# A layer of cross-attention and product-key experts on one core: five tiles of choice in the first stage, one-hots of every fourth block from ScalarE, halved units

## The reference

```
x = x + attention(layernorm(x), ctx, ctx)          # 16 heads of 16, biases, softmax
y = layernorm(x)
xn = y * rsqrt(mean(y*y) + eps) * norm_w
q = (xn @ wq) -> 8 heads x 2 parts x 128
sim = q . keys                                     # 2 x 8 x 64 per token
s1, i1 = top_k(sim[0], 16); s2, i2 = top_k(sim[1], 16)
final_scores, pk = top_k(all 256 sums s1 + s2, 16) # per head
expert = i1 * 64 + i2 at pk                        # one of 4096
hidden = gelu(xn . expert_down[expert]) * relu(final_scores)
x = x + sum over the 8 x 16 choices of hidden * expert_up[expert]
```

## Time and profile before

| what | value |
|---|---|
| median of 3 runs | 1239.93 us (1236.59 to 1240.88) |
| the profiled execution, its own time | 1236.87 us |
| its span | 1235.1 us |
| PE, DVE, ACT, POOL busy | 1061.3, 982.2, 392.6, 535.8 us |
| granted clock of PE, mean | 0.925 of 2.4 GHz |

### The profile page before, as it was taken

One profiled execution on the slowest core, in us unless ns is written; L12 is line 12 of the kernel. 1 busy time (PEld: TensorE's weight loads), 2 busy tenths in 40 slices (PEclk: granted clock), 3 DMA queues, 4 the chain that ended last, 5 costly groups with the idle time before them and its releaser, 6 DMA issues.

```text
span 1235.1 us, 28831 instructions
## 1 busy us (share of the span) xinstructions
PE 1061.3 (86%) x10152; PEld 728.0 (59%) x10152; DVE 982.2 (80%) x4900; ACT 392.6 (32%) x717; POOL 535.8 (43%) x708
## 2 busy tenths in 40 slices
PE   4899987878868685148998999999999999999998
PEld 2444442323213223047777777888878888888887
DVE  4757555959999998588999999999989999964321
ACT  2256544424444361013222222222222222222211
POOL 6320410432111222226565676676766675766400
PEclk9799998888888797557999999999999999999999
DMA  5344313211321100360000000000100010000000
GB/s 167 123 140 142 114 46 121 80 54 42 92 86 41 48 11 26 108 237 2 2 29 16 16 25 16 20 27 9 40 12 25 2 34 16 25 16 24 2 18 9
DMA packets 59925, 63.76 MB, mean 52 GB/s; under 512 B 6882, under 2 KB 56164, under 8 KB 59268
## 3 DMA queue, kind: packets, MB, share of 16 engines
q1 hardware_dynamic: 59780, 61.90, 15.5%
HBM read 42.21 MB, written 19.66 MB: 50 GB/s over the span
## 4 chain that ended last, share of the span: by engine, by line
PE 53%; DVE 26%; POOL 8%; issue 7%; DMA 3%; ACT 2%; SPq 1%; POOLq 0%; DVEq 0%; ACTq 0%
PE bank L1256 50%; DVE mem L1175 4%; POOL mem L783 4%; PE bank L1259 3%; DVE mem L1111 2%; DVE mem L1212 2%; DVE mem L1058 1%; DVE mem L1057 1%; SPq L484 1%; DVE mem L1114 1%; DVE mem L1107 1%; DVE mem L1094 1%; DVE mem L1062 1%; DVE mem L1054 1%; DVE mem L979 1%
## 5 line engine op out<-in xcount | busy, mean ns | idle before, releaser
L1256 PE MATMUL bank<-mem 128*128 128x32 bf16 (+5 forms) x9672 | 1012.3, 276 | 104.2 <-DVE mem L1175 35.6
L1256 PEld LDWEIGHTS bank<-mem 128*128 128x128 bf16 (+3 forms) x9672 | 675.7, 123 | 390.0 <-issue 171.8
L783 POOL TENSOR_TENSOR mem<-mem 128x1536 bf16<-128x1536 bf16 x118 | 325.7, 2761 | 236.4 <-DVE mem L1212 202.7
L1175 DVE TENSOR_REDUCE mem<-bank 128x1 f32<-128x512 f32 x256 | 167.9, 682 | 82.1 <-PE bank L1256 81.9
L888 ACT ACTIVATE mem<-bank 128x512 f32<-128x512 f32 x256 | 148.8, 601 | 203.5 <-PE bank L1256 202.6
L924 ACT ACTIVATE bank<-bank 128x512 f32<-128x512 f32 x128 | 74.5, 582 | 332.3 <-PE bank L1256 332.3
L1212 DVE TENSOR_TENSOR mem<-mem,bank 128x2048 bf16<-128x2048 bf16 x128 | 155.4, 1214 | 0.0
L1259 PE MATMUL bank<-mem 128*128 128x128 f32 (+3 forms) x480 | 75.5, 289 | 66.2 <-POOL mem L695 25.0
L1226 DVE TENSOR_TENSOR mem<-bank,mem 128x512 f32<-128x512 f32 x128 | 87.7, 685 | 49.1 <-ACT bank L924 43.8
L1259 PEld LDWEIGHTS bank<-mem 128*128 128x128 f32 (+3 forms) x480 | 54.9, 142 | 113.5 <-issue 70.8
L932 ACT COPY mem<-bank 128x512 f32<-128x512 f32 x128 | 74.9, 585 | 113.3 <-PE bank L1256 113.3
(11 more groups left out here) (101 smaller groups left out, 678.7 us busy)
## 6 DMA issues: line engine op xcount, KB each, us to landing
mem<-parts_d SPq DMA_DIRECT2D x192, 64.0 KB, 2.3
parts_d<-mem SPq DMA_DIRECT2D x16, 384.0 KB, 2.6
mem<-in_L_ffn_expert_down SPq DMA_DIRECT2D x16, 256.0 KB, 2.8
downT_d<-mem SPq DMA_DIRECT2D x16, 256.0 KB, 3.1
mem<-downT_d SPq DMA_DIRECT2D x4, 1024.0 KB, 8.8
mem<-in_L_ffn_expert_up SPq DMA_DIRECT2D x4, 1024.0 KB, 16.0
tok_d<-mem SPq DMA_DIRECT2D x16, 160.0 KB, 1.8
mem<-tok_d SPq DMA_DIRECT2D x16, 160.0 KB, 2.5
```

The lines of the kernel that those rows point to most:

```text
L783: nc.gpsimd.tensor_tensor(ow[q % 2], i0, i1, ALU.mult).then_inc(ow_rdy, 1)
L1175: nc.vector.tensor_reduce(nmx[g % 2][:, i % TB, i // TB:i // TB + 1], psum[n % 3][:, :], AX.X, ALU.max, negate=True).then_inc(s_max, 1)
L1256: return nc.tensor.matmul(o, l, r, start=first, stop=last)
```

## The change

Four things. `NA` is 5: five tiles are chosen in the first stage, and slots -1, 0 and 1 have five tiles instead of four. Each search, choose and extract is cut into its two rounds, a unit each (34 units of a tile, with the decode a unit of its own), and keys and decode are put at the head of a step, ahead of the one-hots. POOL waits for the small one-hot alone (`oj_rdy`). And the large one-hot of the blocks 3, 7, 11 and 15 of each slot is made by ACT: it negates the 16 high numbers of the block, then for each of its tokens writes |column - number| over 128 columns (`Abs` with the bias from memory), then relu(1 - that) over all 2048; seven tokens in step 1, seven in step 2 and two with the relu in step 3 of each four.

```diff
-        NA = 6
-        TASKS = ([("search", h) for h in range(FH)] +  [("choose", s) for s in range(4)] +
-                 [("keys", 0)] + [("extract", s) for s in range(4)])
+        NA = 5
+        TASKS = ([("search", n) for n in range(2 * FH)] + [("choose", n) for n in range(8)] + [("keys", 0)] +
+                 [("extract", n) for n in range(8)] + [("decode", 0)])
+        HEAD = ("keys", "decode")
+
+        def at_heads(tasks, steps):
+
+            out = []
+            for s, t, kind, i in tasks:
+                s = max(s, out[-1][0]) if out else s
+                if kind in HEAD and out and out[-1][0] == s and s + 1 < steps:
+                    s += 1
+                out.append((s, t, kind, i))
+            return out
...
+        def by_act(q):
+
+            return q % 4 == 3
+
+        def high_of(q):
+
+            return oh[(q - q // 4) % 2]
...
-            run(-1, 3, NA, 4, -1)
+            run(-1, 3, NA, 5, -1)
...
-        FEW = 5
+        FEW = 10
...
-                tasks = [(16 * n // FEW if n < FEW else 16 + 32 * (n - FEW) // (len(tasks) - FEW), *tasks[n][1:])
-                         for n in range(len(tasks))]
+                tasks = at_heads([(16 * n // FEW if n < FEW else 16 + 32 * (n - FEW) // (len(tasks) - FEW), *tasks[n][1:])
+                                  for n in range(len(tasks))], 16 * n_slots)
...
             def weigh(c, par, q):
 
-                pool.wait_ge(oh_rdy, c * 2 + 2)
+                pool.wait_ge(oj_rdy, c + 1)
...
+            FAR = ((), range(0, 7), range(7, 14), range(14, TK))
+
+            def far_from(k, par, q):
+
+                own, step = q // 4 * 4 + 3, q % 4
+                c, n = (k + 1) * 16 + own, (k + 1) * 4 + q // 4
+                if step == 1:
+                    r = 2 * (1 - par) + q // BPT
+                    if q % BPT == 1:
+                        act.wait_ge(tokT_ld[r], ((k + 1) * 2 + q // BPT) * 4 + (16 - 4 * r))
+                    at_least(act, c_mm, c - 3)
+                    nc.scalar.activation(minus, tokT[r][:, own % BPT, 0, :], ACT.Copy, scale=-1.0).then_inc(oh_minus, 1)
+                    act.wait_ge(oh_minus, n + 1)
+                for t in FAR[step]:
+                    nc.scalar.activation(far[:, t, :], row, ACT.Abs, bias=minus[:, t:t + 1]).then_inc(oh_far, 1)
+                if step == 3:
+                    act.wait_ge(oh_far, n * TK + TK)
+                    nc.scalar.activation(far, far, ACT.Relu, bias=1.0, scale=-1.0).then_inc(oh_act, 1)
...
                     if on(kk, 0, 7):
                         gelu(k * 16 + q, q)
+                    if on(kk, -1, 6):
+                        far_from(k, par, q)
...
-                nc.vector.tensor_tensor(oh[q % 2], high.to_broadcast([P, TP, P, PAIR]),
-                                        numbers.unsqueeze(1).to_broadcast([P, TP, P, PAIR]),
-                                        ALU.is_equal).then_inc(oh_rdy, 1)
+                if not by_act(q):
+                    nc.vector.tensor_tensor(high_of(q), high.to_broadcast([P, TP, P, PAIR]),
+                                            numbers.unsqueeze(1).to_broadcast([P, TP, P, PAIR]),
+                                            ALU.is_equal).then_inc(oh_rdy, 1)
...
+                    rest = now["tasks"]
+                    if rest and rest[0][1] in HEAD:
+                        choose_experts(*rest[0])
+                        rest = rest[1:]
                     if on(kk, -1, 6):
                         one_hots(k, par, kk, q)
                     if on(kk1, 0, 7):
                         weigh_hidden(k1, p1, q1)
-                    for task in now["tasks"]:
+                    for task in rest:
                         choose_experts(*task)
...
-                pe.wait_ge(oh_rdy, c * 2 + 2)
+                if by_act(q):
+                    pe.wait_ge(oh_act, (k + 1) * 4 + (q // 4 + 1))
+                else:
+                    pe.wait_ge(oh_rdy, (k + 1) * 12 + (q - q // 4 + 1))
```

More of the change, by code:

```diff
@@ L793, in run @@
                     for tile, kind, i in now["tasks"]:
-                        if (kind, i) == ("extract", 3):
+                        if kind == "decode":
                             weight_parts(tile)
@@ L1100, in make_keys, with extract @@
                 steps.count(nc.vector.tensor_tensor(ik, ik, bits(taken), ALU.bitwise_or))
-            def extract(s):
-                if s == 0:
-                    steps.all()
+            def extract(s, second):
                 both = [(k, o, h) for h in (2 * s, 2 * s + 1) for k, o in ((wkey, kA), (ikey, kB))]
-                a = [steps.count(nc.vector.max(o[:, h, 0:8], k[:, h, :])) for k, o, h in both]
-                b = []
+                if not second:
+                    if s == 0:
+                        steps.all()
+                    a = [steps.count(nc.vector.max(o[:, h, 0:8], k[:, h, :])) for k, o, h in both]
+                    cut.clear()
+                    for n, (k, o, h) in enumerate(both):
+                        steps.after(a[n])
+                        cut.append(steps.count(nc.vector.match_replace(k[:, h, :], o[:, h, 0:8], k[:, h, :], 0.0)))
+                    return
                 for n, (k, o, h) in enumerate(both):
-                    steps.after(a[n])
-                    b.append(steps.count(nc.vector.match_replace(k[:, h, :], o[:, h, 0:8], k[:, h, :], 0.0)))
-                for n, (k, o, h) in enumerate(both):
-                    steps.after(b[n])
+                    steps.after(cut[n])
                     steps.count(nc.vector.max(o[:, h, 8:16], k[:, h, :]))
@@ L1136, in choose_experts @@
                 if kind == "search":
-                    search(tile, i)
-                elif kind == "candidates":
-                    return
+                    search(tile, i // 2, i % 2)
                 elif kind == "choose":
-                    choose(tile, i)
+                    choose(tile, i // 2, i % 2)
                 elif kind == "keys":
                     make_keys(tile)
-                else:
-                    extract(i)
-                    if i == 3:
-                        decode(tile)
+                elif kind == "extract":
+                    extract(i // 2, i % 2)
+                else:
+                    decode(tile)
             def split_first(n):
```

83 lines of the change are left out of this document (52 added, 31 removed).

## The result

| | median us | executions |
|---|---|---|
| before, on the same chip | 1240.41 | 4, 1236.59 to 1247.71 |
| changed | 1253.91 | 4, 1251.38 to 1263.74 |

The ratio is 1.011, 95% interval 1.0069 to 1.015: the change makes the kernel 1.1% slower. The forecast was 1229 us with a range up to 1242, so the result lies outside it and on the other side. The changed kernel's profiled execution took 1254.81 us; its span is 1252.8.

The account below looks back on a forecast made before the run. VectorE was taken to bound slots -1 to 1, TensorE slot 6 and next in slots 2 to 5. From 1236.87 us, -17.7 - 2.5 + 16.5 - 4 = -7.7 gave 1229 us, range 1216 to 1242.

Parts of the forecast that it names:

- part 3: Some large one-hots moved from VectorE to ScalarE: -9.0 us in slots 0 and 1, -4.5 in slot -1, TensorE not waiting.
- Slots 2 to 5, "-4": VectorE relieved there, but TensorE next to bind: 4 us less, to 330 us.
- slot 6, "nothing": Slot that chooses no experts, limited by TensorE alone: no change from 77.16 us.
- Part 1, -17.7: Seam between the stages: with five tiles in the first, the barrier goes from 515.63 to 497.9 us.
- Slot -1, -2.5: Start of second stage: one-hots -4.5, half search +0.85, GpSimd's earlier start meeting VectorE's multiplication +1.2 us.
- Slots 0 and 1, +16.5: Sum of 27.9 - 9.0 - 6.7 + 4.3 us, to some 202 us, VectorE still binding.
- the tile, +27.9: VectorE's price for one more tile beside slots 0 and 1: 28.7 us, less a half search in slot -1.
- The one-hots, -9.0: Slots 0 and 1: VectorE loses eight large one-hots of 1.13 us each to ScalarE.
- The waits for POOL, 9.2: Slots 0 and 1: VectorE's waits at five gates and once for expert numbers, 9.2 us against 4.9 before.
- Keys at the head, -6.7: Slots 0 and 1: keys' first instruction no longer meets GpSimd's multiplication, saving four times 1.66 us.
- Rival B: No change, 1233 to 1236 us, if VectorE idles 13 to 16 us in slots 0 and 1; chance 0.22.
- Rival C: Slower: GpSimd falls behind in slots 0 and 1, delaying gates and keys, 16 us more, 1245 us; chance 0.14.

Follow-up runs that it names:

- e2: Kernel before, with the output's copy (take_out) moved ahead of the coefficients' copy in step 2: 1236.36 us, ratio 0.9956 to before.
- e4: Kernel before, with seven unused Abs on ScalarE ahead of the output's copy in each of slots 0 to 6: 1255.99 us, ratio 1.0103 to before.
- e3: Changed kernel with all large one-hots on VectorE again, the output's copy left where it was: 1254.64 us, ratio 1.0068 to before.
- e1: Changed kernel with the output's copy right behind gelu in step 2, ahead of the seven Abs: 1239.35 us, ratio 0.9958 to before.
- e9: e1 with GpSimd waiting also for VectorE's large one-hots; one execution: slot -1 48.07 us instead of 45.07, slots 0 and 1 8.1 more.
- e5: e1 with six tiles in the first stage again and four beside slots -1 to 1: 1219.54 us, ratio 0.9826 to before.
- e8: e1 with keys and decode behind the one-hots instead of at a step's head; one execution: slots 0 and 1 205.25 us, 2.2 more.

## Why the prediction was wrong

**The step that failed is in part 3: "the product on PE that needs the one-hots comes a step later, so it waits for none of it".** It followed one consumer, the reader of the one-hots, and its sum of "the most at one step" took the step with the long instruction. But a queue delays what stands behind, whoever reads it. In step 2 the seven pieces are 2.1 us ahead of `take_coef` and of `take_out`, and the output's copy has a reader without a step of slack. The rows to see it in were there: the kernel before shows PE waiting for L937 1.16 us in slot 6 (and six times, 7.0 us, from slot 2 on), so the copy was already on the path and each microsecond ahead of it had to come out at the other side. One of the prediction's own signs of being wrong, that ScalarE's blocks make PE wait, came true, though not through the one-hots' reader. The text asked whether ACT binds; the question was who on ACT is already late. The Trainium skill (PSUM — Partial Sum Buffer, Engine vs sequencer instructions) states the rule in half a sentence, that ScalarE's, VectorE's and GpSimd's queues are strictly first in, first out; the timelines above agree with it.

**Slots 2 to 5, "-4", and slot 6, "nothing"**, fell with it: +11.9 and +4.2. Of the 4.2, 1.3 are the longer wait and 2.9 the lower clock behind it, for which the sum had no term. With the copy put first the same slots take 329.0, near the forecast's 330; but e2 reaches 330.9 without the change. DVE's relief, the reason given for the 4 us, is worth 1.9 there, by one execution of each.

**Part 1, -17.7**, came as 515.63 - 501.8 = 13.8. The barrier fell with the landing of the attention's last store, as said, and from there to the first search it was 12.5 us before and 12.8 after; the attention's own end moved. In the profiled executions the last store of xn was issued at 495.60 in the kernel before, and at 499.53 in the changed one, where it landed 2.3 later and the first load behind the barrier follows:

```profile
499.53 0.62 SPq L542 DMA_DIRECT2D xn_d<-mem  x1
502.13 0.36 SPq L620 DMA_DIRECT2D mem<-tok_d  x1
```

Four other kernels with the first stage of before issue it at 498.65 to 507.45, and all five-tile ones at 499.33 to 501.27. The execution of before that was profiled had simply been quick in its attention. The prediction said it lay 3.1 us under the median, and took it as base nevertheless; 1232 was the better centre. What makes the attention's length vary wasn't settled (the granted clock from 340 to 400 us was 0.89 before and 0.80 after, 0.80 in e2 and e4 too). It may be why the medians are spread more than the stretches; with one trace of each kernel that isn't shown.

**Slot -1, -2.5**, came as -2.7 by terms that cancel. ACT's one-hots brought 46.56 - 45.07 = 1.5 of the 4.5 (e3 against e1): DVE had 3.7 us less to do, but stood 2.1 us before its small one-hots (L1269), 1.4 of them until PE was through with a block, where e3 has no such wait. And POOL's earlier start brought 3.0 instead of costing 1.2 (e9 against e1): 1.7 in DVE's own multiplications, 1.2 in waits for PE. The meeting that it was charged with is small: the ten multiplications take 9.8 us in e1 and in the changed kernel, 9.5 in the kernel before, 11.5 in e9.

**Slots 0 and 1, +16.5**, came as +17.8. By DVE's own account the sum holds: it was busy 13.2 us more (forecast 27.9 - 9.0 - 6.7 = 12.2) and idle 4.6 more (forecast 4.3). The parts, each against e1: the tile, +27.9, measured 29.9 (e5, where PE comes close to binding, so it may be more). The one-hots, -9.0, measured -6.5. The waits for POOL, 9.2, measured 9.4. Keys at the head, -6.7, measured -2.2 (e8): the keys' first instruction did fall from 2232 ns to a mean of 901, but most of that came without the heads. POOL's start measured -8.1; 6.2 of it are waits at the gates and for the numbers, which the gates' term already took as shortened, and 0.6 lies in the keys.

**Balance without the wait.** e1 against e2, both with the copy first: slot 0 begins 18.2 us earlier (forecast 20.2), slots 0 and 1 take 17.7 more (16.5), slots 2 to 5 take 1.9 less (4). That is -2.4 instead of -7.7, and the medians say 3 us the other way, inside their intervals. Rival B, "what is moved comes back whole", names this outcome. But its condition wasn't met: DVE's waits for POOL in slots 0 and 1 are 9.4 us, by the count that gave 5 before and 9 in the forecast, and B was to hold from 13. Rival C had the right sign of the result by luck, from the wrong place: the gates did no more than the forecast said, and the keys' first instructions 1.7 us more in all. No rival named ACT's queue, and none named a cost of PE's clock in slots where the clock was 1.00.

**The move of the tile itself** was costed nearly right and judged too kindly. Some 15 to 18 us at the seam were bought with 28 to 30 beside slots 0 and 1; the change looked good only because savings that don't depend on it were set against it. With six tiles they are kept, and e5's span is 15.7 us under e1's (1216.5 and 1232.2).

## What to carry to other kernels

Before work is put on an idle engine, list what stands behind the insertion point in its queue and how long each reader there already waits: an engine that is idle two thirds of the time can still have one instruction that another engine waits for, and moving that one instruction ahead of the new work returned 14.6 us of medians here (1253.91 to 1239.35). Price the parts of a change one by one against the stretch that they touch, and ask of a move whether it is a gain without the other parts. And take a wait of PE at its length only while the granted clock behind it stays up: look at both levels in the rows.
